# Cross-attention block: waits in slots 3 to 8 and 64 rearranged, and the loop over eight slots written out

## The reference

```
Q = split_heads(x @ Wq + bq);  K = split_heads(ctx @ Wk + bk);  V = split_heads(ctx @ Wv + bv)
attn = softmax(Q K^T / sqrt(32));  ctx2 = attn V, heads merged
out = layer_norm(ctx2 @ Wo + bo + x, gamma, beta)
```

## Time and profile before

| what | value |
|---|---|
| median of 3 runs | 609.81 us (609.68 to 613.28) |
| the profiled execution's own time | 609.58 us |
| its span | 607.8 us |
| PE busy | 587.6 us, 97% of the span |
| DVE, POOL, ACT busy | 477.2, 445.8, 401.8 us |
| DMA | 129.56 MB, mean 213 GB/s |

### The profile page before, as it was taken

How to read it: one execution, slowest core, us unless ns; L and a number is a source line. 1 busy time by engine, 2 the same in 40 slices (tenths; PEclk the granted TensorE clock), 3 DMA queues, 4 the chain that set the end, 5 groups by cost and what they waited for, 6 DMA issues and landing times.

```text
span 607.8 us, 11567 instructions
## 1 busy us (share of the span) xinstructions
PE 587.6 (97%) x3102; PEld 426.3 (70%) x3102; DVE 477.2 (79%) x775; ACT 401.8 (66%) x837; POOL 445.8 (73%) x396
## 2 busy tenths in 40 slices
PE   8999989999999999999999999999999999999793
PEld 6877757677777777777777777777777777777362
DVE  6535568788888888888888888888888888888776
ACT  5622553567777777777777777777777777776562
POOL 1364252377888888888889888888888888987785
PEclk9999999999999999999999999999999999999998
DMA  8868897979898898988887988898898989796513
GB/s 297 330 223 209 244 218 172 247 175 229 214 213 225 211 229 207 233 230 216 208 221 209 221 216 220 216 207 223 218 218 220 232 214 217 212 218 174 149 54 138
DMA packets 93455, 129.56 MB, mean 213 GB/s; under 512 B 50000, under 2 KB 50000, under 8 KB 93424
## 3 DMA queue, kind: packets, MB, share of 16 engines
q1 hardware_dynamic: 73888, 93.27, 61.6%
q10 hardware_dynamic: 19536, 35.92, 21.5%
HBM read 53.94 MB, written 24.35 MB: 129 GB/s over the span
## 4 chain that ended last, share of the span: by engine, by line
PE 91%; POOL 3%; DVE 2%; ACT 1%; ACTq 1%; issue 1%; DMA 1%; DVEq 0%; SPq 0%; POOLq 0%
PE p_q L650 28%; PE p_o L737 27%; PE p_s L688 10%; PE p_v L699 9%; PE p_a L674 6%; PE pk L323 5%; PE p_o L113 3%; PE pvv L113 1%; PE p_a L754 1%; DMA cx<-in_ctx_t 1%; POOL prob L1195 1%; PE p_q L754 0%; POOL xl L1201 0%; POOL wol L1260 0%; ACT ch L835 0%
## 5 line engine op out<-in xcount | busy, mean ns | idle before, releaser
L810 ACT ACTIVATE prob<-p_s 77x512 f32<-77x512 f32 x256 | 141.6, 591 | 82.6 <-PE p_s L688 74.3
L1070 DVE TENSOR_REDUCE nm<-p_a 128x4 f32<-128x308 f32 x256 | 117.8, 469 | 53.0 <-PE p_a L674 49.5
L1201 POOL TENSOR_TENSOR xl<-xt,xh 128x512 fp32r<-128x512 f32 x60 | 77.4, 1291 | 102.5 <-ACT xh L817 102.4
L1011 DVE TRANSPOSE_TENSOR_REDUCE part<-prob 96x64 f32<-96x2048 f32 x64 | 146.7, 2292 | 0.1
L650 PE MATMUL p_q<-xl,wqh 128*128 128x512 f32 x256 | 101.0, 395 | 0.0
L650 PE MATMUL p_q<-xh,wqh 128*128 128x512 f32 x256 | 101.0, 395 | 0.0
L650 PE MATMUL p_q<-xh,wql 128*128 128x512 f32 x256 | 100.9, 394 | 0.0
L737 PE MATMUL p_o<-woh,ch 128*128 128x512 f32 x240 | 96.1, 400 | 0.9 <-DVE y L1003 0.9
L737 PE MATMUL p_o<-wol,ch 128*128 128x512 f32 x240 | 94.7, 395 | 0.0
L737 PE MATMUL p_o<-woh,cl 128*128 128x512 f32 x240 | 94.6, 394 | 0.0
L688 PE MATMUL p_s<-z,ks 97*77 97x512 f32 x256 | 93.8, 407 | 0.4 <-ACT prob L810 0.4
(11 more groups left out here) (140 smaller groups left out, 946.9 us busy)
## 6 DMA issues: line engine op xcount, KB each, us to landing
z<-qh SPq DMA_DIRECT2D x256, 128.0 KB, 3.0
z<-ql SPq DMA_DIRECT2D x120, 128.0 KB, 4.2
xn<-in_x ACTq DMA_DIRECT2D x60, 256.0 KB, 3.6
out_dram<-y SPq DMA_DIRECT2D x60, 256.0 KB, 4.1
xt<-in_x_t ACTq DMA_DIRECT2D x58, 256.0 KB, 4.3
ks<-k_high SPq DMA_DIRECT2D x32, 154.0 KB, 4.6
cx<-in_ctx_t SPq DMA_DIRECT2D x4, 616.0 KB, 5.1
k_high<-kth SPq DMA_DIRECT2D x4, 616.0 KB, 3.6
```

Source lines behind the costliest of these rows:

```text
L810: nc.scalar.activation(prob[0:S2, g.k % 2, j, :], p_s[j % 2][0:S2, :], ACT.Exp, scale=SCALE).then_inc(prob_ready, 1)
L1011: nc.vector.tensor_reduce(part[:, g.k % 2, :], prob[0:KP, g.k % 2, :, :].rearrange("p h (i r) -> p (h i) r", r=DK), AX_X, ALU.add, apply_t ...
L1070: nc.vector.tensor_reduce(nm[:, t, g.k % 2:HALF:2], p_a[t % 2][:, 0:HC * S2].rearrange("p (h k) -> p h k", k=S2), AX_X, ALU.max, negate=Tr ...
L1201: nc.gpsimd.tensor_tensor(xl[:, i, n.k % KC, :], xt[:, n.k % 2, :], xh[:, i, n.k % KC, :].bitcast(F32), ALU.subtract).then_inc(xl_ready, 1)
```

## The change

The loop in `run` is replaced by straight code for all slots. The two quarters of Wo of slot 4 are loaded in slot 3. DVE's `add_bv` moves to the front of its slot. In slot 8 ACT issues one residual tile and bo at the front; the second residual tile goes to its regular place behind the first two exps, and gamma and beta to the end of the slot, with a semaphore for bo of its own and a wait for gamma and beta before the first `scale`. In slot 64 PE waits before the values for one division fewer (59, not 60), and for 60 before the first sums.

```
-            loop_from, loop_to = 2, NG // PAIR - 1
-            for u in range(loop_from):
-                for k in range(PAIR):
-                    slot(Slot(u, k))
-            with engine.Fori(loop_from, loop_to) as u:
-                for k in range(PAIR):
-                    slot(Slot(u, k))
-            for k in range(PAIR * loop_to, end):
+            for k in range(end):
                 slot(Slot(k // PAIR, k % PAIR))
...
-                for half in range(2):
-                    if g.back(WO_SLOTS[half] - 1).is_first():
-                        load_wo(2 * half)
-                        load_wo(2 * half + 1)
+                if g.back(WO_SLOTS[0] - 1).is_first():
+                    for kc in range(KC):
+                        load_wo(kc)
...
             def sums(g):
 
                 pe.wait_ge(part_ready, g.over(1, 1))
+                pe.wait_ge(cx_ready, NG - LAG_PV)
...
                 if not g.valid(NG):
-                    pe.wait_ge(cx_ready, v.over(1))
+                    pe.wait_ge(cx_ready, v.over(1, -1) if v.over(1) == NG - LAG_PV else v.over(1))
                     values(v)
...
                 if g.back(ROWS_SLOT).is_first():
                     act.wait_ge(v_summed, VT)
                     load_residual(Slot(0, 0))
-                    load_residual(Slot(0, 1))
-                    for row, src in ((bo, "bo"), (gamma, "ln_gamma"), (beta, "ln_beta")):
-                        act.dma_start(row[:], a[src].partition_broadcast(P)).then_inc(rows_in, 16)
+                    act.dma_start(bo[:], a["bo"].partition_broadcast(P)).then_inc(bo_in, 16)
...
-                if g.back(LAG_NORM - 2).valid(NS) and not g.back(ROWS_SLOT - 1).is_first() and not g.back(ROWS_SLOT).is_first():
+                if g.back(LAG_NORM - 2).valid(NS) and not g.back(ROWS_SLOT - 1).is_first():
                     load_residual(g.back(LAG_NORM - 2))
...
+                if g.back(ROWS_SLOT).is_first():
+                    for row, src in ((gamma, "ln_gamma"), (beta, "ln_beta")):
+                        act.dma_start(row[:], a[src].partition_broadcast(P)).then_inc(rows_in, 16)
                 for kc in wo_in_slot(g):
                     split_wo_high(kc)
...
                 v, m = g.back(LAG_PV), g.back(LAG_NORM)
+                for i in v_in_slot(g.back(1)):
+                    add_bv(i)
                 if m.valid(NS) and not g.valid(NG):
                     add_residual(m)
...
-                for i in v_in_slot(g.back(1)):
-                    add_bv(i)
                 if m.valid(NS) and g.valid(NG) and g.k % 2 == 1:
                     add_residual(m)
...
             def scale(m):
+                if m.is_first():
+                    pool.wait_ge(rows_in, 32)
...
             def add_bo(m):
                 if m.is_first():
-                    pool.wait_ge(rows_in, 48)
+                    pool.wait_ge(bo_in, 16)
```

More of the change, by code:

```diff
@@ L426, in attend @@
         stored = [sem(f"stored{i}") for i in range(4)]
-        rows_in = sem("rows_in")
+        rows_in, bo_in = sem("rows_in"), sem("bo_in")
         x_last_in = [sem(f"x_last_in{t}") for t in range(QT)]
```

## The result

The changed kernel takes 606.77 us as the median of 13 executions, the kernel before 610.42 us as the median of 13. The medians differ by 3.65 us. The ratio is 0.9932, with a 95% interval from 0.9913 to 0.995, which is 4.1 us less (3.1 to 5.3), where 5.9 were forecast; 606.77 lies above the range that ended at 606.0. One of the 13 took 2033.81 us and is left out of the ratio; the others lie between 604.12 and 609.92. The profiled execution is one of 606.88 us, with a span of 605.0.

A forecast was written before the change was run, and what follows sets the result against it. TensorE was taken as the bound, busy 587.6 of 607.8 us. Gains of 2.25 (slots 5 and 6), 1.4, 0.3 and 1.94 sum to 5.9 off 609.58: 603.7, or 603.9 us as median; range 601.6 to 606.0.

The forecast's parts named there:

- Slot 6, the wait: With add_bv ahead of the divide, PE's 2.7 us wait becomes a 1.8 us wait for exp behind the divide.
- Slot 6, its value: Moving add_bv in slot 6 gains 2.65 us, with 1.7 us lost to the lower clock counted before the change.
- Slot 5: Earlier Wo loads delay the maxima's DMAs: a new PE wait costing 0.4 us, bounds 0 to 1.0, 2 at the outside.
- Slot 8: Fewer ACT issues ahead of q_high remove PE's wait and gain 1.4 us over slots 7 to 9.
- Slots 9 to 15: These slots ran 0.36 us above the yardstick, put down to a late add_bo; 0.3 us counted as gain.
- The loop: Straight code for slots 15 to 57 brings pairs to 16.24 us and gains 1.94 us, bounds 0 and 2.0.
- Instruction fetch: Rival: fetching straight code for slots 16 to 55 stops PE, up to 30 us, giving 634 us; chance 0.05.
- Slot 64: Moving PE's divide wait is worth 0, bounds 0 and 2.4; PE waits 2.1 us before the sums instead.
- from there to the end the same time as before: After PE's new wait in slot 64, the rest takes as long as before, 32.7 us from 575.07.
- the granted clock at 1.00 in all windows: Expected in the profile after: with slot 6's wait near 1.8 us, the clock stays at full throughout.
- the clock falls all the same: Rival: clock falls behind the 1.8 us wait in slot 6 or 2.1 in slot 64, costing 1.7 us: 605.6; chance 0.2.

The follow-up runs named there:

- first experiment: The changed kernel with Wo loaded in two slots again (3 and 4): 605.76 us, ratio 0.9929.
- early split: The changed kernel with Wo's last two quarters loaded behind the maxima in slot 4 and split earlier, in slot 5, by ScalarE and GpSimd: 603.21 us, ratio 0.9875.
- the unrolled one: The kernel before with only the loop written out as straight code: 608.35 us, ratio 0.9974.
- the old wait in slot 64: The changed kernel with PE again waiting for the division of chunk 59 before the values of chunk 60: 606.68 us, ratio 0.995.
- the tail's add_bo: The changed kernel with Wo's last quarters loaded and split earlier, plus GpSimd's add_bo first in its slot from slot 64 on: 601.19 us, ratio 0.9843.

## Why the prediction was wrong

The mechanisms stood, and two sizes were off, both too favourable. Point by point:

- **Slot 6, the wait.** Right. Forecast 1.8 us for exp behind the divide, measured 1.70; slot 6 is 9.00 us. That the earlier load of Wo gains nothing was right to within 0.3 us (first experiment), and that it is the order behind the loads that holds the divide too (early split).
- **Slot 6, its value: the step that failed.** "2.65 us" contained 1.7 us for the clock, taken from one execution. Four profiles with the old slot 6 (three of the kernel before, one of the unrolled one) have 11.57, 10.00, 11.32 and 10.00 us, a mean of 10.72. Against 9.00 the gain is 1.0 us where the clock stays up and 2.6 where it falls: 1.7 on these four. The prediction weighed a fall in the new kernel as a rival and took the fall in the old one as certain: 2.65 us stood where the moved wait alone is worth 1.0.
- **Slot 5.** Right in kind, too small. Forecast 0.4 us, with 1.0 and "2 at the outside" as bounds; the waits were 1.28, 0.82 and 1.26 us in the three profiles with all four loads in slot 3 (the third is that of the old wait in slot 64), and the slot is longer by 1.1 us as their mean. The maxima's issue came 0.6 us later against the first matmul of slot 5, not the forecast 1.05. From its end to PE's use, (73.95 + 2.95) to 80.35, they now take 3.4 us, against at most 2.7 before: at least 0.8 us more in the first profile and 0.3 in the second. That the loads cause this is shown by the first experiment. That it is the 512 KB ahead of the maxima in the queue, which had been left for the outside bound, fits and is not shown, since no view has the landings of these four DMAs.
- **Slot 8.** Right: 16.27 us for the pair where 16.3 was forecast.
- **Slots 9 to 15.** The 0.3 us were put down to a late add_bo. With that add_bo as late as ever three of five profiles have 48.8 and two 49.1; with the early one eight profiles have 48.7 to 49.0. The gain is 0.1 us at most, and 49.09 was mostly chance.
- **The loop.** Right: slots 15 to 57 take 341.1 to 341.6 us in nine profiles with straight code and 342.9 to 343.1 in four with the loop, 1.7 us as the difference of the means; the time of the kernel with this part alone has 1.6. Instruction fetch cost nothing that shows: the page after has 25 packets on queue 8 where the page before has 14, and 27 on queue 14, which the prediction did not count, where it had 17; the pairs are at 16.24 to 16.26.
- **Slot 64.** Right that the edit is worth nothing, and where PE would wait instead (2.1 forecast, 1.9 measured). But "from there to the end the same time as before" failed: the tail was 56.32 and 56.16 us. Of the first, 0.4 us came ahead of DVE's y, from ScalarE's residual issue of 1.01 us where it was 0.68 (0.92 in the second), and 0.8 behind it, with the fall of the clock. So "the granted clock at 1.00 in all windows" failed as well.

The sum, against the forecast of 603.9 and the measured 606.77 us: 0.6 from the median of the kernel before, which was 609.81 in three runs and 610.42 in thirteen; 0.9 from slot 6; 0.7 from slot 5 (1.1 as the mean, not 0.4); 0.2 from slots 9 to 15; 0.1 to 0.3 from the loop. These make 2.6. The tail would add 0.5, if the mean of 55.85 us over four profiles with the new wait and the same order on GpSimd (56.32, 56.16, 55.85, 55.06) and 55.39 over six with the old one (55.11, 55.12, 55.09, 56.67, 55.12, 55.25) are taken as different; their spread doesn't allow that to be called shown. With the clock left aside the stretches give 1.0 from slot 6, 1.4 from slot 8, 0.1 from slots 9 to 15 and 1.7 from the loop, less 1.1 in slot 5: 3.1 us. The times agree. A straight line through time against mean granted clock, for 56 executions of the kernel before and 24 of the changed one, gives 610.3 and 607.1 us at a clock of 0.990, which is 3.2 us apart (an estimate from the runs on record).

The rival "the clock falls all the same" came true, but in the profile after not behind either of the waits that it named: the fall is at 569.4 us, behind PE's wait of 1.23 us for y, and costs some 0.8 us, not 1.7. Its chance of 0.2 was too low: between slot 64 and the last work of PE there was a fall in all ten profiles of the changed and the other kernels, and in one of the three of the kernel before.

What stays open is whether the new arrangement of slot 64 makes a costly fall more likely. The clock fell in all seven profiles with the new wait and in four of six with the old one. With the old one the fall cost nothing in two profiles (55.12 and 55.09 us), 0.1 us in a third (55.25) and 1.6 us in a fourth (56.67).

## What to carry to other kernels

Read the granted clock of a stretch before a wait is priced, and price the wait without it: what an idle stretch costs in clock is a draw per execution, and two more profiles of the same kernel show what belongs to the kernel. Before a load is moved forward, look at what stands behind it in the same queue, small transfers with an early reader above all, and at whether the engine that consumes it would even take it sooner. When a wait is taken off an engine, follow the order of work on each of the others to the next gate; where reordering one of them (here GpSimd's two low parts) removes the cause, it gave more than moving the wait had: 603.21 against 607.15 us on one chip, of which some 1 us is the wait of slot 5 that the same edit takes away, and 601.19 with the tail's add_bo as well.

## What was not expected of the hardware

The same wait of 2.63 to 2.69 us in the same kernel came with the lower clock in two profiles (granted 0.71 and 0.57 from 88 to 92 us) and not in a third (1.00), which is worth 1.3 to 1.6 us of 610. The Trainium skill (TensorE: Matmul & The Clock Gate, The HAM clock gate) says that the monitor runs freely and isn't reset by the kernel's start, so that the same kernel meets it at another phase each time. The three profiles fit that, since one and the same wait had different outcomes; where the monitor stood in each of them they don't show.

And after the first pass of the loop of eight slots no packet of instructions came. In the kernel before queue 8 shows for 165 to 240 us, in which the first pass falls,

```profile
q8 instruction: 4, 0.07, 0.4%
```

and between 240 and 505 us, in which the other four run, neither instruction queue has any. After the change the queues show in that stretch:

```profile
q8 instruction: 12, 0.20, 0.3%
q14 instruction: 15, 0.12, 0.2%
```

These cost nothing that shows in the pairs of slots.
